# A gated linear attention block on one core: half of k's transposes, the normalisation of x, the weighting of v and the attention stores change their engines

## The reference

```
xn  = layernorm(x)
q   = elu(xn @ Wq) + 1        k = elu(xn @ Wk) + 1        v = xn @ Wv
a   = sigmoid(xn @ Wa + ba + 2)                    # one decay per token and head
S_t = a_t * S_(t-1) + k_t v_t^T                    # per head, along the sequence
z_t = a_t * z_(t-1) + k_t
o_t = (q_t . S_t) / (q_t . z_t + 1e-6)
x1  = x + o @ Wo
out = x1 + (layernorm(x1) @ CB^T) * SCB / 127 + bias
```

## Time and profile before

| | |
|---|---|
| time, median of 3 runs | 1962.0 us (1961.59 to 1962.97) |
| the profiled execution: its own time | 1964.17 us |
| its span, first to last instruction | 1962.4 us |
| granted TensorE clock, mean | 0.998 |
| first phase, until about | 1430 us |

### The profile page before, as it was taken

How to read it: one execution, slowest core, us unless ns; L and a number is a source line. 1 busy time by engine, 2 the same in 40 slices (tenths; PEclk the granted TensorE clock), 3 DMA queues, 4 the chain that set the end, 5 groups by cost and what they waited for, 6 DMA issues and landing times.

```text
span 1962.4 us, 69099 instructions
## 1 busy us (share of the span) xinstructions
PE 1939.8 (99%) x26926; PEld 1690.4 (86%) x26926; DVE 1645.8 (84%) x2918; ACT 687.0 (35%) x1288; POOL 392.9 (20%) x368
## 2 busy tenths in 40 slices
PE   8999999999999999999999999999999999999999
PEld 6888888898888988888889888888878888888887
DVE  8788888888888888888888888888787777777776
ACT  5333344333433343334333433334432222222221
POOL 3222222232222222332222223322010000000000
PEclk9999999999999999999999999999999999999999
DMA  6334444444444444444344444444477666666664
GB/s 216 89 93 97 98 111 100 109 104 104 104 97 98 102 109 100 107 106 108 95 98 100 113 95 109 106 111 124 91 165 175 161 161 161 160 161 161 160 161 117
DMA packets 596067, 237.40 MB, mean 121 GB/s; under 512 B 432064, under 2 KB 546240, under 8 KB 596032
## 3 DMA queue, kind: packets, MB, share of 16 engines
q1 hardware_dynamic: 560896, 204.94, 44.2%
q10 hardware_dynamic: 35136, 32.00, 5.7%
HBM read 168.59 MB, written 51.97 MB: 112 GB/s over the span
## 4 chain that ended last, share of the span: by engine, by line
PE 96%; DVE 2%; issue 1%; DMA 1%; SPq 0%; POOL 0%; POOLq 0%; ACT 0%; DVEq 0%
PE G L1332 54%; PE DS L1290 17%; PE NUM L1290 8%; PE NUM L1401 4%; PE SC L1454 3%; PE DS L1433 3%; PE NUM L1415 3%; PE SC L1280 2%; PE DS L1474 1%; DVE w_lo L917 0%; DMA norm_rows<-moments 0%; DVE w_lo L949 0%; DMA abc<-decay_rows 0%; DMA product_rows<-pT 0%; DVE D L1114 0%
## 5 line engine op out<-in xcount | busy, mean ns | idle before, releaser
L1332 PE MATMUL G<-w_hi,xT_hi 128*128 128x512 f32 x1024 | 406.9, 397 | 0.9 <-DVE w_lo L917 0.9
L1332 PE MATMUL G<-w_lo,xT_hi 128*128 128x512 f32 x1024 | 400.1, 391 | 0.0
L1332 PE MATMUL G<-w_hi,xT_lo 128*128 128x512 f32 x1024 | 398.7, 389 | 0.0
L738 ACT ACTIVATE relu_t<-G 128x512 f32<-128x512 f32 x256 | 153.1, 598 | 452.6 <-PE G L1332 450.4
L1332 PE MATMUL G<-xT_hi,w_hi 128*128 128x256 f32 x1024 | 290.2, 283 | 0.2 <-DVE w_lo L917 0.2
L1332 PE MATMUL G<-xT_lo,w_hi 128*128 128x256 f32 x1024 | 289.8, 283 | 0.0
L1332 PE MATMUL G<-xT_hi,w_lo 128*128 128x256 f32 x1024 | 289.7, 283 | 0.0
L1332 PEld LDWEIGHTS G<-w_hi,xT_hi 128*128 128x128 f32 x1024 | 192.4, 188 | 42.9 <-DVE xT_lo L910 1.0
L1332 PEld LDWEIGHTS G<-w_hi,xT_lo 128*128 128x128 f32 x1024 | 192.3, 188 | 41.4
L1332 PEld LDWEIGHTS G<-w_lo,xT_hi 128*128 128x128 f32 x1024 | 192.5, 188 | 35.5
L706 ACT ACTIVATE w_hi<-at_rows 128x512 fp32r<-128x512 f32 x128 | 73.9, 625 | 381.2 <-PE DS L1290 352.2
(11 more groups left out here) (137 smaller groups left out, 3609.2 us busy)
## 6 DMA issues: line engine op xcount, KB each, us to landing
abc<-decay_rows SPq DMA_DIRECT2D x256, 128.0 KB, 3.3
pbc<-product_rows SPq DMA_DIRECT2D x256, 128.0 KB, 3.1
attn_cols<-attn SPq DMA_DIRECT2D x512, 64.0 KB, 2.2
at_rows<-attn_cols ACTq DMA_DIRECT2D x244, 128.0 KB, 2.8
xt<-in_x SPq DMA_DIRECT2D x64, 256.0 KB, 3.2
x_in<-in_x SPq DMA_DIRECT2D x64, 256.0 KB, 3.0
out_rows<-xt SPq DMA_DIRECT2D x64, 256.0 KB, 3.0
xT_in<-in_xT SPq DMA_DIRECT2D x31, 512.0 KB, 4.4
```

The lines of the kernel that those rows point to most:

```text
L738: act.activation(relu_t[buffer][:, :], bank[:, :], ACT.Relu)
L1332: made = nc.tensor.matmul(to, lhs, rhs, start=(n == 0), stop=(n == len(passes) - 1))
```

## The change

* PE transposes k of half 0 only (8 instead of 16 transposes a step). k of half 1 is transposed in blocks by DVE in the chunk's own step (`turned_k1`, behind the second `x_lo`), and SP moves it into kT with four DMAs (`place_k`). `scores` waits for both `kT_copied` and `kT_loaded` of the chunk before.
* In an odd step SP now issues `store_decays`, `place_k`, the wait for the decays' landing, `spread_decays(0)`, `products(1)`, `products(0)`, `load_columns`; in an even step `place_k` comes behind `products(0)`.
* The stores of the attention output go from SP's queue to POOL's.
* DVE normalises the columns of x, with two instructions of 128 x 1024 in the even step. ACT copies the spread statistics to `norm_c` first, in another order (`norm_by_rows`). The elements of x are no longer touched by POOL.
* `weighted_v(1)` goes from DVE (one instruction) to ACT (eight, one per head), and `carried_on(0)` from DVE (one) to ACT (four).
* DVE does the elu of k half 1 ahead of `scaled_q`.

The semaphores' declarations, changed counts and unchanged lines are left out here.

```diff
     xT_in = sb("xT_in", [128, KT, 2 * C])
-    norm_b = bias_b[:, :].rearrange("p (c s a) -> p a s c", s=2, a=2)
+    norm_c = sb("norm_c", [128, 4 * C])
+    norm_b = norm_c[:, :].rearrange("p (a s c) -> p a s c", s=2, a=2)
+    x_tiles = xT_in[:, :, :].rearrange("p k (s c) -> p k s c", s=2)
     stats = sb("stats", [128, 2, 6])
...
-        def store_rows(r, n, count):
-            here = chunk_at(n)
-            sp.wait_ge(attn_ready[r], count)
-            for c in range(2):
-                for half in range(2):
-                    q = 64 * c + SQ * half
-                    sp.dma_start(cols_of(here)[c, r, :, :, SQ * half:SQ * half + SQ],
-                                 attn[q:q + SQ, U * r:U * r + U].rearrange("f (b t) -> f b t", t=SQ))\
-                        .then_inc(attn_stored[r], 16)
         def load_x(n, b):
...
                                      pT[g:g + H, :]).then_inc(decay_stored, 16)
-                sp.wait_ge(decay_stored, p80[1])
...
                     .then_inc(norm_loaded, 16)
+            def place_k():
+                sp.wait_ge(scores_ready, one[0])
+                if exists(i - 1):
+                    wait(sp, kT_loaded, k64[-1])
+                sp.wait_ge(k_turned_ready, one[0])
+                for g in range(4):
+                    q = SQ * g
+                    sp.dma_start(kT[:, twos(1), q:q + SQ],
+                                 k_turned[q:q + SQ, :].rearrange("f (b t) -> f b t", t=SQ)).then_inc(kT_loaded, 16)
...
                 ffn_weights()
-            if exists(i - 2) and not (isinstance(i, int) and i == NC + 1):
-                store_rows(1, i - 2, one[-2])
+            if gates:
+                store_decays()
+            if b == 1 and exists(i):
+                place_k()
+            if gates:
+                sp.wait_ge(decay_stored, p80[1])
+                if not exists(i):
+                    sp.wait_ge(w_lo_ready, KT)
+                spread_decays(0, next_pair, 0)
             if b == 1 and exists(i):
...
             if gates:
-                store_decays()
-                if not exists(i):
-                    sp.wait_ge(w_lo_ready, KT)
-                spread_decays(0, next_pair, 0)
                 products(0, coming)
...
                 products(0, coming)
+            if b == 0 and exists(i):
+                if isinstance(i, int) and i == 0:
+                    sp.wait_ge(w_lo_ready, KT + 2)
+                place_k()
             if isinstance(i, int) and i == NC - 1:
...
                 load(1, 1)
-            if exists(i - 1):
-                store_rows(0, i - 1, one[-1])
             if isinstance(i, int) and i == NC - 4:
...
+        def store_rows(r, n, count):
+            here = n
+            if not isinstance(n, int):
+                here = pool.snap(n)
+                pool.compute_val(here)
+            pool.wait_ge(attn_ready[r], count)
+            for c in range(2):
+                for half in range(2):
+                    q = 64 * c + SQ * half
+                    pool.dma_start(cols_of(here)[c, r, :, :, SQ * half:SQ * half + SQ],
+                                   attn[q:q + SQ, U * r:U * r + U].rearrange("f (b t) -> f b t", t=SQ))\
+                        .then_inc(attn_stored[r], 16)
         def step(i, pair, b):
+            one = counts(pool, i, 1, (-2, -1))
             if b == 0 and exists(i + 2):
-                pairs = counts(pool, pair, 1, (0, 1))
-                p16 = counts(pool, pair, 16, (0,))
-                inverse_deviation(pairs[1])
-                x4 = xT_in[:, :, :].rearrange("p k (s c) -> p k s c", s=2)
-                pool.wait_ge(xT_loaded, p16[0])
-                pool.wait_ge(norm_loaded, p16[0])
-                for kt in range(KT):
-                    made = pool.tensor_tensor(x4[:, kt, :, :], x4[:, kt, :, :], norm_b[:, 0, :, :], ALU.subtract)
-                made.then_inc(xT_centred, 1)
-                pool.wait_ge(xT_centred, pairs[0])
-                for kt in range(KT):
-                    made = pool.tensor_tensor(x4[:, kt, :, :], x4[:, kt, :, :], norm_b[:, 1, :, :], ALU.mult)
-                made.then_inc(xT_normal, 1)
-            if isinstance(i, int) and i == NC:
+                inverse_deviation(counts(pool, pair, 1, (1,))[1])
+            if isinstance(i, int) and i == NC + 1:
                 inverse_deviation2(1)
+            if exists(i - 2) and not (isinstance(i, int) and i == NC + 1):
+                store_rows(1, i - 2, one[-2])
+            if exists(i - 1):
+                store_rows(0, i - 1, one[-1])
+            if isinstance(i, int) and i == NC + 1:
                 pool.wait_ge(wf_loaded, 16 * KT)
...
                 inverse_deviation2(counts(pool, i, 1, (0,))[0])
+            if isinstance(i, int) and i == 3:
+                store_rows(1, NC - 1, NC)
...
                 act.wait_ge(kT_ready, one[0])
-                held = slice(0 if exists(i) else GH, PT if exists(i - 1) else GH)
                 for a in range(2):
-                    act.activation(kT[:, held, stretch(a)], turned_k[a][:, held, :], ACT.Copy)\
-                        .then_inc(kT_copied[a], 1)
+                    made = act.activation(kT[:, twos(0), stretch(a)], turned_k[a][:, twos(0), :], ACT.Copy)
+                made.then_inc(kT_copied, 1)
+            def norm_by_rows():
+                act.wait_ge(norm_loaded, p16[0])
+                wait(act, xT_normal, pairs[-1])
+                act.activation(norm_b, bias_b[:, :].rearrange("p (c s a) -> p a s c", s=2, a=2), ACT.Copy)\
+                    .then_inc(norm_ready, 1)
...
-            if exists(i) or exists(i - 1):
+            def weighted_v1():
+                act.wait_ge(v_ready[1], one[0])
+                act.wait_ge(D_ready[1], one[0])
+                wait(act, delta_ready[1], one[-1])
+                for h in range(HH, H):
+                    made = act.activation(vw[:, h, :], v1[1 - b][:, h, :], ACT.Copy, scale=D[:, h, L - 1:L])
+                made.then_inc(vw_ready[1], 1)
+            def carried_on0():
+                act.wait_ge(pc_ready, one[0])
+                act.wait_ge(state_ready[0], one[-1])
+                for j in range(GH):
+                    made = act.activation(S_part[:, j, :], S[b][:, j, :], ACT.Copy, scale=pc[:, j, 0:1])
+                made.then_inc(carry_ready[0], 1)
+            if exists(i):
                 copy_kT()
...
                 copy_num(1)
+            if exists(i) and exists(i - 1):
+                carried_on0()
             if gates and not first:
...
                 q_parts(0)
+                if exists(i):
+                    weighted_v1()
                 q_parts(1)
...
             elif b == 1 and exists(i):
+                weighted_v1()
                 chunk_decay(i, one, None, c32[0])
             elif exists(i):
+                if exists(i + 2):
+                    norm_by_rows()
                 q_parts(2)
                 q_parts(3)
+                weighted_v1()
                 if closing:
...
                                                ALU.min, ALU.add).then_inc(k_ready[r], 1)
+            def turned_k1():
+                if exists(i - 1):
+                    wait(dve, kT_loaded, k64[-1])
+                dve.wait_ge(k_ready[1], one[0])
+                nc.vector.transpose(k_turned[:, :].rearrange("p (x j t) -> p x j t", x=4, t=SQ),
+                                    k[:, U:2 * U].rearrange("p (j f x) -> p x j f", f=SQ, x=4))\
+                    .then_inc(k_turned_ready, 1)
...
                                         ALU.mult).then_inc(qs_ready[r], 1)
+            def over_tiles(a):
+                return norm_b[:, a:a + 1, :, :].broadcast_to([128, KT, 2, C])
+            def centred_columns():
+                dve.wait_ge(xT_loaded, x16[0])
+                dve.wait_ge(norm_ready, pairs[0])
+                nc.vector.tensor_tensor(x_tiles, x_tiles, over_tiles(0), ALU.subtract).then_inc(xT_centred, 1)
+            def normal_columns():
+                dve.wait_ge(xT_centred, pairs[0])
+                nc.vector.tensor_tensor(x_tiles, x_tiles, over_tiles(1), ALU.mult).then_inc(xT_normal, 1)
...
                 decays()
+            if exists(i) and not second:
+                elu_k(1, 0)
             for r in (1, 0):
...
                     x_lo(1, pairs[1], xT_in[:, :, tokens(1)])
-                if not second:
-                    elu_k(1, 0)
+                turned_k1()
             last = isinstance(i, int) and i == NC - 1
...
                 decay_matrix(1)
-                weighted_v(1, one[0], one[-1], o)
             if last:
...
             elif exists(i + 1):
+                if exists(i + 2):
+                    centred_columns()
                 elu_q(2, 1)
                 decay_matrix(0)
+                if exists(i + 2):
+                    normal_columns()
                 elu_q(3, 0)
...
                 elu_k(0, 1)
-            for r in (1, 0):
-                if exists(i - r) and exists(i + 1 - r):
```

(40 more changed lines are left out.)

## The result

The changed kernel takes **2038.55 us** (median of 4 runs, 2036.2 to 2042.85) against 1962.49 us of the kernel before in the same session: ratio 1.0389, 95% interval [1.0376, 1.0402]. It is slower, as forecast, but by 76 us and not by 20, and 2038.55 lies above the range (1948 to 2012). The profiled execution took 2042.85 us, the longest of the four; its span is 2041.2 us.

What follows compares the result with a forecast made beforehand. The prediction took PE's instructions to bound the first phase. Its terms, -15.8 (transposes) + 34.1 (waits at scores) + 3.5 (end of phase one) - 1.4 (start) = +20.4 us on the median 1962.0, gave 1982 us, range 1948 to 2012.

Steps and rivals of the forecast that it cites:

- PE's transposes: PE, steps 1 to 63: eight fewer transposes save 0.25 us a step, 15.8 us less in all.
- DVE and ACT: Loop pairs: DVE gains 2.4 us, to 40.6 of 43.3; ACT gains weightings 2.0 and carries 1.0; no cost on the path.
- rival D: Stores on POOL stretch DVE, PE waits for k: +1 us a pair on top of the forecast, 2013; chance 0.04.
- hidden: POOL's 16 attention stores a pair, taken at 1 us each, 16 us a pair, cost no time up to 2.7 us each.
- the lower of my two bounds: Price of one attention store on POOL: 0.63 us from the same transfer on SP; the upper was 3.1 us.
- rival C: POOL becomes the bound at 3.1 us a store, 50.3 us a pair: +200 us, 2160; chance 0.07.
- a slip of 2.6 us: SP, odd step: the last pbc load lands later, +1.0 us for place_k and +1.6 for products(1).
- It waits 1.1 us: PE at scores, behind late pc, v and kT on ACT: 1.1 us in 31 odd steps, +34.1 us.
- has the wait itself as cover: DVE, odd step: carried_on(1) and weighted_v(0), late behind pc, are covered by PE's wait at scores.
- The upper end of that wait: PE's wait at scores with the longest wait for pbc, 1.9 us (1.3 more): 2.3 us.
- The end of the first phase: Step 63: k half 1's transfers land at 1430.1, PE is at scores at 1426.47: +3.5 us.
- The start: PE's first wait, for DVE's k: DVE's part gets 1.4 us shorter, -1.4 us.

Runs made afterwards that it cites:

- e5_place_mid: The changed kernel with the odd step's place_k moved between products(0) and load_columns: 1958.55 us, ratio 0.9974 to the kernel before.
- e4_stores_sp: The changed kernel with all attention stores back on SP's queue in their two old places: 2017.34 us, ratio 1.0287 to the kernel before.
- e6_mid_sp: As e5_place_mid, with the attention stores also back on SP's queue: 1956.65 us, ratio 0.9966 to the kernel before.
- e11_r0_sp: The changed kernel with only the four r = 0 attention stores back at the end of SP's step: 2019.56 us, ratio 1.029.
- e2_products_early: The changed kernel with products(1) alone put back ahead of store_decays in SP's odd step: 2067.13 us, ratio 1.052.
- e9_last_v_dve: As e6_mid_sp, but in step 63 DVE weights v of heads 8 to 15 in one instruction instead of eight on ACT: 1955.94 us, ratio 0.9957.
- e10_last_k_pe: As e9_last_v_dve, with k of heads 8 to 15 of step 63 transposed by PE in step 64 and copied by ACT: 1952.30 us, ratio 0.9938.

## Why the prediction was wrong in size

**PE's transposes, right.** SC L1359 is x8 and 0.39 us in the chain, and e5_place_mid shows 0.49 us a pair.

**DVE and ACT, right.** The groups of one pair of the changed kernel, shapes apart, which answer to the earlier trace rows:

```profile
L1190 DVE TENSOR_TENSOR_SCAN D<-abc,eye 128x512 f32<-128x512 f32 x4 | 4.8, 1202 | 0.4 <-DMA abc<-decay_rows 0.4
L1087 DVE SCALAR_TENSOR_TENSOR qT<-exp_t,relu_t 128x512 f32<-128x512 f32 x4 | 2.8, 688 | 0.9 <-ACT exp_t L765 0.9
L1079 DVE STREAM_TRANSPOSE k_turned<-k 128x512 f32<-128x512 f32 x2 | 2.2, 1101 | 0.0
L1159 DVE TENSOR_TENSOR xT_in<-xT_in,norm_c 128x1024 f32<-128x1024 f32 x1 | 1.2, 1194 | 0.0
```

The transposes cost 1.10 for 1.08, the long instructions 1.19 and 1.20 for 1.24. The elus are back at 0.69 from 1.00, so stores on GpSimd's queue don't stretch DVE: rival D is out. By the Trainium skill, "SBUF — State Buffer", Who interferes with whom, a VectorE instruction with two SBUF inputs contends with a GpSimd instruction that reads SBUF. The trace agrees: with GpSimd's arithmetic on x gone the elu is at 688 ns, although GpSimd is busy for 301 us of the loop, nearly all of it issuing stores. Eight weightings on ACT span 2.02 us for 2.0.

**GpSimd, the price below what I took, and wrong in the word "hidden".** A store takes 635 ns on its queue, the lower of my two bounds, where I took 1 us; POOL is busy for 19%, and rival C is out. But I had asked only what a store costs the queue that issues it, not whom its packets meet. GpSimd issues the r = 0 stores 4.5 to 1.8 us ahead of the last pbc load, where SP used to issue them behind it. e4_stores_sp prices that at 21 us (2038.55 - 2017.34) with `place_k` where the change has it; with `place_k` moved, e6_mid_sp finds no difference. The rule stands in the Trainium skill, in "Trainium Kernel Development and Optimization", Key Constraints: DMAs from all queues run on the same 16 engines and interleave, and another issuing engine saves issue time alone. The waits agree: ACT waits for pbc 3.98 us in the mean with the stores among the loads, 3.51 and 3.43 with them behind (e4_stores_sp, e11_r0_sp: 113.3 in 33).

**SP, the sum nearly right, its terms wrong.** I forecast a slip of 2.6 us, +1.0 for `place_k` and +1.6 for `products(1)`. Measured: 2.9 (9.88 - 6.97), which is +3.75 and -0.85. I took the end of `place_k` against the abc loads as they stood, at 726.43, without asking what held them there: the early `products(1)`, blocked on DVE for 77.5 us in all. That wait was in the trace. Two errors cancelled, and had I tried to repair the change by my own terms I would have moved `products(1)`, which makes it worse (e2_products_early).

**The term that failed: "It waits 1.1 us".** The mechanism and the threshold were right: pc had to be copied 11.73 us after the copy of v (733.4 - 721.67), and the measured one is 719.64 - 1.72 - 706.27 = 11.65. But pc comes later, for 0.3 us more slip and for landings that GpSimd's stores lengthen. PE waits 1.92 us, 61.5 in 32 waits where I had 34.1 in 31. A further 0.30 us goes at `delta(0)`, 20 times, for DVE's `carried_on(1)` and `state(1)`; I had written that `carried_on(1)` "has the wait itself as cover"; it did not in these 20 steps. (The upper end of that wait was also added up short: 1.09 + 1.28 is 2.4, not 2.3.)

**The clock, left out of the loop.** The two pairs of stretches below each show a wait and the 4 us behind it (PEclk is the third number from the end):

```profile
396.00:397.50 1.50, 0.00 (x0) 0.00 (x0) 0.49 (x2) 1.37 (x5) 0.00 (x0) 1.00 0.52 164
397.50:401.50 4.00, 3.90 (x157) 3.93 (x160) 3.76 (x9) 1.35 (x5) 0.00 (x0) 0.57 0.00 0
...
767.00:768.60 1.60, 0.13 (x8) 0.16 (x12) 0.73 (x2) 1.60 (x5) 0.00 (x0) 1.00 0.07 20
768.60:772.60 4.00, 3.71 (x165) 3.35 (x165) 3.76 (x9) 1.73 (x6) 0.00 (x0) 1.00 0.01 2
```

At 397.5 the clock is at its half level for most of 4 us, which costs 4.00 x 0.43 = 1.7 us. The rows of 50 us from 100 to 1450 us name 1.00 but for eight, which lack 0.25 of a row together: 12.5 us, seven or eight such stretches. Against the loop of e5_place_mid, without waits, PE's busy time is 17.8 us longer (1230.46 - 1212.68); the clock explains 12.5 of them, the other 5 stay unexplained.

**What took the time out of the range.** The measured wait of 1.92 us lies within the 0.6 to 2.3 that the prediction allowed. Put into its sum it gives 1962 - 13.7 + 31 x 1.92 = 2008 us, below the top of 2012. The other 30 us are what the sum had at nothing or too small: 17.8 of slower PE in the loop, most of it the half clock, 5.9 at `delta(0)`, and 8.8 more at the end of the first phase. The half clock behind a wait stood in the prediction for the start alone; nothing of it was carried to the waits that it forecast in every pair.

**The loop adds up:** -13.8 (28 pairs x 0.49) + 62.1 idle + 17.8 slower = 66.1.

**The end of the first phase, +12.3 for +3.5.** I had counted the transfers of k (taking them away gives 3.6 us between the medians of e9_last_v_dve and e10_last_k_pe, 1.9 between their profiled stretches, 620.79 and 618.89), but not PE's 2.7 us wait for ACT's eight weightings in step 63, nor the inverse deviation behind GpSimd's stores, nor the half clock behind these waits. How the 8.8 us divide among these is not shown: e9_last_v_dve takes the first away and is hardly faster. **The start, -1.4, did not show:** it was +0.4 to the scores of step 4, with the first waits for pc already in it; in e5_place_mid it is -1.4 (120.03 against 121.40), though the clock, 0.99 there for 0.97, has its part in that.

## What to carry to other kernels

When a transfer moves to another queue, ask not only what its issue costs but which transfers its packets now run beside, and who waits for those. When a queue's order changes, first find what set its old times: a blocked instruction that goes away gives its wait back, and a slip counted from the old times is wrong in each part even where the sum comes out. Place a transfer by its deadline, between those that are due before it and those that are not: four DMAs cost nothing in the loop between the two, 80 us more ahead of the loads that PE waited for, and 28 us more behind a large load that nobody waited for yet.

## What the runs showed of the hardware that was not expected

* With four stores of 64 KB issued from GpSimd's queue just ahead, the last pbc load took over a microsecond longer: 4.95 us to the copy of pc in the kernel before with the stores moved, 3.2 without (731.85 - 728.64). SP's wait for the landing of a 2 KB store grew too, from 1.7 to 3.3 us (52.3 and 97.6 in 30).
* The half clock does not follow the length of the wait: 2.02 us at 397.6 was followed by it, 3.49 us at 768.5 was not.
